# A macaron block on eight cores: layer-norm stages one round earlier, a square moved to GpSimd, attention weights staged in a buffer of their own, causal masks moved to VectorE

## The reference

```python
x = x + 0.5 * ffn(layernorm(x), W_fc, W_proj)
x = x + attn(layernorm(x), W_q, b_q, W_k, b_k, W_v, b_v, W_o, b_o)   # 16 heads of 64, causal
x = x + 0.5 * ffn(layernorm(x), W_fc, W_proj)                        # same weights

def ffn(x):
    h = square(relu(x @ W_fc.T))          # 1024 -> 4096
    y = h @ W_proj.T                      # 4096 -> 1024
    mem = 0; spikes = 0
    for _ in range(5):                    # each step needs the one before it
        reset = mem > 1
        mem = 0.9 * mem + y - reset
        spikes += mem > 1
    return spikes / 5
```

## Time and profile before

| what | value |
|---|---|
| median of 5 runs | 5807.53 us (5806.66 to 6020.43) |
| profiled execution, its own time | 5804.35 us |
| its span on the slowest core (core 6) | 5802.8 us |
| spans of the 8 cores | 5786.1 to 5802.8 us |
| busy share of PE, DVE, ACT, POOL | 66%, 32%, 37%, 5% |
| mean granted TensorE clock | 0.805 |

### The profile page before, as it was taken

One profiled execution on the slowest core, in us unless ns is written; L12 is line 12 of the kernel. 1 busy time (PEld: TensorE's weight loads), 2 busy tenths in 40 slices (PEclk: granted clock), 3 DMA queues, 4 the chain that ended last, 5 costly groups with the idle time before them and its releaser, 6 DMA issues.

```text
span 5802.8 us, 65741 instructions; the slowest of 8 cores (5786.1 to 5802.8 us)
## 1 busy us (share of the span) xinstructions
PE 3857.2 (66%) x24162; PEld 2282.6 (39%) x24194; DVE 1884.8 (32%) x2563; ACT 2150.5 (37%) x2527; POOL 262.3 (5%) x574
## 2 busy tenths in 40 slices
PE   0288888888536653666635664566663888888885
PEld 0166666666413311111113330111211666666664
DVE  0134444544421152211122115221111344445444
ACT  1134434444312213555631220446561344344443
POOL 0000000000000001111100000111110000000000
PEclk9999999999868765666767885556766999999998
DMA  4500000000030001001021001000104000000000
GB/s 173 196 15 30 15 30 30 30 27 19 22 116 15 15 1 44 29 29 29 1 88 49 16 8 44 29 10 20 29 1 152 16 30 22 24 30 30 30 15 22
DMA packets 140922, 222.38 MB, mean 38 GB/s; under 512 B 3376, under 2 KB 118064, under 8 KB 138560
## 3 DMA queue, kind: packets, MB, share of 16 engines
q1 hardware_dynamic: 116480, 117.45, 6.5%
q0 software_dynamic: 12864, 58.78, 3.0%
q10 hardware_dynamic: 11264, 41.95, 2.0%
HBM read 151.05 MB, written 67.11 MB: 38 GB/s over the span
## 4 chain that ended last, share of the span: by engine, by line
PE 41%; DVE 22%; ACT 16%; issue 10%; DMA 7%; POOL 3%; DVEq 1%; ACTq 0%; POOLq 0%; SPq 0%
PE pw L188 39%; ACT ae L989 5%; POOL ae L1014 2%; ACT f1xbf L693 2%; ACT f3xbf L693 2%; DVE f1m L689 2%; DVE f3m L689 2%; DVE f1m L684 2%; DVE f3m L684 2%; PE pw L192 2%; DVE s_cden L880 2%; DMA f1wst<-wfc 1%; ACT ae L999 1%; DVE awvu L1091 1%; ACT aq L809 1%
## 5 line engine op out<-in xcount | busy, mean ns | idle before, releaser
L188 PE MATMUL pw<-f3lnx,f3wfc 128*128 128x256 bf16 x4096 | 882.8, 285 | 122.9 <-ACT f3h L617 73.3
L188 PE MATMUL pw<-f1lnx,f1wfc 128*128 128x256 bf16 x4096 | 880.2, 284 | 123.5 <-ACT f1h L617 73.7
L188 PE MATMUL pw<-f3h,f3wpr 128*128 128x256 bf16 x4096 | 861.4, 280 | 0.4
L188 PE MATMUL pw<-f1h,f1wpr 128*128 128x256 bf16 x4096 | 859.5, 280 | 0.4
L188 PE MATMUL pw<-ae,av 128*65 128x512 bf16 (+3 forms) x1664 | 486.8, 404 | 553.7 <-POOL ae L1014 269.0
L989 ACT ACTIVATE ae<-pw,s_negc,c_f 128x1024 bf16<-128x1024 f32 x448 | 524.9, 1198 | 373.3 <-PE pw L192 301.6
L188 PEld LDWEIGHTS pw<-f3lnx,f3wfc 128*128 128x128 bf16 x4096 | 408.5, 102 | 208.5 <-issue 152.9
L188 PEld LDWEIGHTS pw<-f1lnx,f1wfc 128*128 128x128 bf16 x4096 | 407.1, 101 | 208.7 <-issue 154.0
L188 PEld LDWEIGHTS pw<-ae,av 128*65 128x65 bf16 x1664 | 164.3, 137 | 812.8 <-issue 797.2
L188 PEld LDWEIGHTS pw<-f3h,f3wpr 128*128 128x128 bf16 x4096 | 408.5, 100 | 130.1 <-issue 65.2
L188 PEld LDWEIGHTS pw<-f1h,f1wpr 128*128 128x128 bf16 x4096 | 408.2, 100 | 129.6 <-issue 64.3
(11 more groups left out here) (145 smaller groups left out, 4239.5 us busy)
## 6 DMA issues: line engine op xcount, KB each, us to landing
ax<-x1t SPq DMA_DIRECT2D x32, 1024.0 KB, 7.8
f1x<-xt SPq DMA_DIRECT2D x16, 1024.0 KB, 5.5
x1t<-f1x SPq DMA_DIRECT2D x16, 1024.0 KB, 4.6
x2t<-ax SPq DMA_DIRECT2D x16, 1024.0 KB, 6.8
f3x<-x2t SPq DMA_DIRECT2D x16, 1024.0 KB, 5.4
out<-f3x SPq DMA_DIRECT2D x16, 1024.0 KB, 4.4
f1wst<-wfc POOLq DMA_DIRECT2D x4, 2048.0 KB, 8.5
f1wst<-wfc ACTq DMA_DIRECT2D x4, 2048.0 KB, 7.9
```

What stands on the lines that cost most here:

```text
L188: sp=stop: eng.matmul(o, l, r, start=st, stop=sp))
```

## The change

There are three edits.

1. In the feed-forward stages the spike thunks are shared out over R1 to R4 (they were over R1 to R5). Stages 1 to 6 of the next tile's layer norm are emitted one round earlier, and stage 1, the square, is given to GpSimd.
2. In attention the weights pass through a new tile astg of two 1 MB halves and no longer through x_in, in the order q0, k0, q1, k1 and so on, and each cast 1 MB piece has its own dependency.
3. The two mask multiplications of each diagonal chunk go from GpSimd to VectorE.

```diff
                         if r == 1:
                             extra = stages[0]()
+                        elif r == 5:
+                            extra = stages[2]()
                         elif r == 6:
-                            extra = stages[2]()
-                        elif r == 7:
                             extra = stages[4]()
                     emit_mms(h_mms(r), y_mms(r - 1), extra,
-                             front=(r in (6, 7)))
+                             front=(r in (5, 6)))
                     relu_round(r)
-                    if pending_spike[0] and r <= 5:
-                        k_n = max(1, -(-len(pending_spike[0]) // (6 - r)))
+                    if pending_spike[0] and r <= 4:
+                        k_n = max(1, -(-len(pending_spike[0]) // (5 - r)))
...
                     if stages is not None:
-                        if r == 5:
-                            stages[1]()
+                        if r == 4:
+                            stages[1]("gpsimd")
+                        elif r == 5:
+                            stages[3]()
                         elif r == 6:
-                            stages[3]()
-                        elif r == 7:
                             stages[5]()
                             stages[6]()
```

```diff
+            astg = mksbuf(ph, "astg", [128, 2 * 2048], F32)
...
+                for idx, (nm, ddr, wt, ch) in enumerate(stjobs):
+                    pp = idx % 2
+                    sg = astg[:, pp * 2048:(pp + 1) * 2048]
+                    sgB = B(f"astg{pp}")
+                    kb.dma("gpsimd" if pp == 0 else "scalar",
...
+                    kb.op("vector", lambda e, w=wt, ch=ch, sg=sg:
+                          e.tensor_copy(
+                              w[:, ch * 2048:(ch + 1) * 2048], sg),
+                          reads=(sgB,), writes=(B(f"{nm}c{ch}"),))
...
                                 for off in (u0, 512 + u0):
-                                    kb.op("gpsimd", lambda e, off=off,
+                                    kb.op("vector", lambda e, off=off,
```

More of the change, by code:

```diff
@@ L743, in emit_attn @@
             atmp = mksbuf(ph, "atmp", [128, 2048], F32)
+            astg = mksbuf(ph, "astg", [128, 2 * 2048], F32)
+            bufs["astg0"] = Buf("astg0")
+            bufs["astg1"] = Buf("astg1")
             c_bvb = mksbuf(ph, "abvb", [1, D], BF16)
@@ L755, in emit_attn @@
                 wvb = mksbuf(qkvstack, f"awv{b}", [128, 8192], BF16)
-                for nm, ddr, wt in ((f"awq{b}", d_wq, wqb),
-                                    (f"awk{b}", d_wk, wkb),
-                                    (f"awv{b}", d_wv, wvb)):
+                for nm in (f"awq{b}", f"awk{b}", f"awv{b}"):
                     for ch in range(4):
[L760 to L771, removed]
+                        bufs[f"{nm}c{ch}"] = Buf(f"{nm}c{ch}")
@@ new lines, in emit_attn @@
+                stjobs = [(f"awq{b}", d_wq, wqb, 0), (f"awk{b}", d_wk, wkb, 0),
+                          (f"awq{b}", d_wq, wqb, 1), (f"awk{b}", d_wk, wkb, 1),
+                          (f"awq{b}", d_wq, wqb, 2), (f"awk{b}", d_wk, wkb, 2),
+                          (f"awq{b}", d_wq, wqb, 3), (f"awk{b}", d_wk, wkb, 3),
+                          (f"awv{b}", d_wv, wvb, 0), (f"awv{b}", d_wv, wvb, 1),
+                          (f"awv{b}", d_wv, wvb, 2), (f"awv{b}", d_wv, wvb, 3)]
+                for idx, (nm, ddr, wt, ch) in enumerate(stjobs):
[3 more added lines that the diff above has]
+                    kb.dma("gpsimd" if pp == 0 else "scalar",
+                           sg.rearrange("p (c n) -> p c n", c=2),
+                           ddr.ap().rearrange("(c p) n -> p c n",
+                                              p=128)[:, 2 * ch:
+                                                     2 * ch + 2, :],
+                           writes=(sgB,))
+                    kb.op("vector", lambda e, w=wt, ch=ch, sg=sg:
+                          e.tensor_copy(
+                              w[:, ch * 2048:(ch + 1) * 2048], sg),
+                          reads=(sgB,), writes=(B(f"{nm}c{ch}"),))
@@ L804, in emit_attn @@
                                           start=(dk == 0), stop=(dk == 7),
-                                          reads=(B(nm), B("alnx")))
+                                          reads=(B(f"{nm}c{dk // 2}"),
+                                                 B("alnx")))
                             for hj in range(4):
@@ L826, in emit_attn @@
                                       start=(dk == 0), stop=False,
-                                      reads=(B(f"awv{b}"), B("alnx")))
+                                      reads=(B(f"awv{b}c{dk // 2}"),
+                                             B("alnx")))
                         for hf in range(2):
@@ L930, in emit_attn @@
                     del bufs[n]
+                    for ch in range(4):
+                        del bufs[f"{n}c{ch}"]
                 corestack = ExitStack()
@@ L1206, in emit_attn @@
             for n in ("aq", "ak", "av", "ax0", "ax1", "alnx", "axbf",
-                      "axsq", "aab", "arw", "atmp", "abvb"):
+                      "axsq", "aab", "arw", "atmp", "abvb", "astg",
+                      "astg0", "astg1"):
                 del bufs[n]
```

## The result

The changed kernel has a median of 5960.37 us over 6 runs (5945.93 to 6111.47), against 5807.53 before. It is slower by a ratio of 1.0275, 95% interval 1.0213 to 1.0338. In some executions, of any kernel, the cores of a die run part of the time at a lowered clock, which lifts the medians (that of all ten executions of the kernel before to 5951.47), so single times given from here on are of executions without it: 5945.7 to 5949.3 us for this kernel, 5803 to 5807 for the one before, +140 us. The profiled execution (6016.82 us) is read on core 2 (span 5952.4 us) in f1 and attention, and on core 5 in f3, where their stores come as evenly as in the kernel before.

What follows compares the result with a forecast made beforehand. No engine is full; the spike chain's latency up to xsq's first sum sets each feed-forward tile. Feed-forward +217, masks -52, weights -15 gave +150 on 5804.35, forecast as 5956 us, range 5855 to 6050 (5905 to 6010 at 0.65).

Steps and rivals of the forecast that it cites:

- the masks' gain: Attention's diagonal chunks: masks on VectorE take 0.55 us a pair, not 1.02; -52 us in all.
- the clock given back at R0: Feed-forward, next tile's R0: without the lnx wait its matmuls no longer run at the lower clock, -2.4 us a tile.
- First sum later: Feed-forward tile: the first sum of xsq on PE starts at 1136.0, 3.7 us later than before.
- lower clock behind the long wait: Feed-forward R5: PE has stood nearly still for 14 us, so the round pays +2.4 us a tile.
- no wait for lnx: Feed-forward, next tile's R0: lnx is made during R7 and ready when wanted, -2.3 us a tile.
- The price of the square: Feed-forward square on GpSimd: 4.46 us, plus 1.1 us held by line 704 on DVE.
- dear-square rival: Feed-forward square takes 6.83 us on GpSimd and is held for all of line 704: +98 us, 6054; chance 0.12.
- Tile 0: First tile of each feed-forward stage: no Signs before it, early square, loses 7.7 us of waits and clock; twice, -15.
- 1.2 us x 48 = -58: Attention, qs = 1, 2, 3: each of 48 head pairs ends 1.2 us earlier through faster masks, -58 us.
- attention wins: Rival: PE's mask waits in attention vanish, gaining more than the feed-forward stages lose; about 5806 or 5785 us; chance 0.08.
- Head and qs = 0: Attention: masks behind W_o's casts at each core part's head cost +3, twice, +6; at qs = 0 tail_a's hold nets 0.
- Weights: Start of attention: x no longer waits for weight buffers, so statistics come 7.5 us earlier, twice, -15 us.

Runs made afterwards that it cites:

- e6: Kernel before with spike thunks shared out as 5, 4, 4, 4 and the rest over R1 to R5, one Sign per round: 5800.97 to 5806.67 us, ratio 1.0004.
- e5: Changed kernel with the square of x written to a tile of its own, xs2, instead of xsq: 5711.79 us in one execution.
- e7: Changed kernel with line 704, the store and the next load emitted behind the row statistics: 5915.13 and 5918.1 us.
- e2: Kernel before with only the mask multiplications moved from GpSimd to VectorE: 5731.16 us, ratio 0.9898.
- e3: Kernel before with only the new weight staging and its dependencies by piece: 5787.6 to 5791.6 us, ratio 0.9961.
- e9: Changed kernel with norm and spikes interleaved, square in its own tile on ScalarE, broadcasts in R4, normalising behind R4 to R7: 5252.33 and 5260.09 us.

## Why the prediction was right or wrong

The directions and the waits came as forecast. Two terms were mis-sized most, and the granted clock stands in both: the masks' gain, and the clock given back at R0. Their errors had opposite signs.

**The mechanism of edit 1 held.** The claim was that the first sum of xsq waits for the spike chain, so that a round moved from ahead of it to behind it is a round lost. The trace shows it (first sum 41.9 us behind S0, 38.2 before; line 700 34.7 us behind S0, 34.8 before), e6 shows the sum's time is not PE's to change (38.1 us with another order of waits), and e5 shows the reverse: with the square off the chain, the tile is back at 82 us.

**Term by term, a tile** (means of tiles 1 to 13 of f1, core 2). First sum later: forecast 3.7, measured 3.7. All behind it: forecast +4.6, measured 48.3 - 42.9 = +5.4. This is the mis-sized part of edit 1, +0.8 a tile, 21 us over the 26 tiles between the first and last stores:

| term behind the first sum | forecast | measured |
|---|---|---|
| one more round of 64 matmuls | +6.9 | +7.0 |
| lower clock behind the long wait | +2.4 | +2.0 (5.7 us for the 25 matmuls, 3.7 at full clock) |
| no wait for lnx | -2.3 | -2.5 |
| its lower clock gone | -2.4 | -1.1 |

The term that failed is the last, "minus 2.4 us of lower clock". It was read from one tile and taken for all. Behind the first sum the tiles before take 41.8, 43.2 or 43.3 us: three of the 13 lose nothing to the clock, six lose 1.4 us in R6, behind the 3.0 us wait that "cost no clock", and only four lose 1.5 us in R0. The price of 2.3 to 2.4 in R0 was itself too high, since it set 26 matmuls in 5.09 us against 0.107 us each, while R0's matmuls at full clock take 0.13 (39 in 5.10 us, one tile earlier).

**The price of the square was right by luck, by two errors.** Forecast 4.46 alone and 1.1 held, 5.56 us; measured 3.60 (e5, e7) and 2.11, 5.71. GpSimd is faster on one wide operation than its 128-column row and DVE's fixed part suggest, and was held for nearly all of line 704. The dear-square rival was right on the hold and wrong on the price. The Trainium skill (GPSIMD Engine Reference, Performance versus the Vector engine) gives 4497 ns for a 2048-column fp32 tensor_tensor add on GpSimd; this product of one tile with itself took 3600, and for this form the measurement decides. Its Key points say that GpSimd contends with VectorE's instructions that have two SBUF inputs; the trace agrees: 2.11 us lost beside one of 2.29.

**Tile 0** gave 4.8 us in f1 where I had 7.7. In f3 9.6 us went, but its start also holds the load of the weights, which differs by some us from core to core.

**Masks: the wrong size, and the largest miss.** Forecast -52; e2 measured -76. The step that failed is "1.2 us x 48 = -58". The 1.2 us were right as far as they went (1.28 in the pair shown). Over the 48 pairs it came to 1.8 us each in e2. What I left out is the clock: where the gap ahead of tail_pe is shorter, the broadcasts can run at 2.4 and not 1.2 GHz, 0.9 us more in the pair shown. That pair is a good one: in the mean the broadcasts won 0.3 us in e2, and the stretch ahead of them 1.5 and not 1.2. The clock of that stretch rose too, from 0.68 to 0.90, so the other 0.3 may be the clock's as well; that is argued, not isolated. I had counted the clock in the feed-forward and not here; I had it only in the rival "attention wins", which it did not bring about, as the feed-forward loss of 239 stayed more than twice attention's gain. Head and qs = 0 cost 7 us in e2 where +6 was forecast, at the places named: the first product with v came 4.0 and 4.2 us later in the two batch elements (8 cores), and at qs = 0 tail_a's wait rose by 1.0 us.

**Weights: -15 forecast**, statistics 10.2 us earlier after the barrier in the mean of the cores (7.5 forecast), -16 in e3. Of the 4 us that I took for lost to traffic, 1.2 were lost.

**The sum** missed by only 10 us by luck, because the errors had both signs: feed-forward +239 (forecast +217), attention -98.5 on core 2 (-67), -103 in the mean of the cores. My own conditions for being wrong were tiles under 83 us (they took 90.3) and core parts over 80 us shorter; per element the query blocks 1 to 3 gave 44 to 46 us.

## What to carry to other kernels

- When PE waits in several places of a loop, ask which event is set by a chain with no slack. Work moved from ahead of that event to behind it adds its full length, and a wait in front of it is worth nothing to remove (e6: 4.8 us moved, 0 won).
- A buffer that two chains share can be the tie that makes a wait. Look for it before moving work: one more tile of 4 KB per partition turned +140 us into -93 (e5), and with the norm then laid where its inputs are ready, into -552 (e9).
- Price a shorter or longer PE gap twice: once for its time, and once for the matmuls behind it at 1.2 or 2.4 GHz. Take the second price as a mean over many tiles: the same 25 matmuls behind nearly the same wait took 3.7 us in one tile and 5.15 in another.

## What the runs showed of the hardware

- A GpSimd product of two 2048-column fp32 operands (the same tile twice) into bf16 took 3.60 us alone and 5.71 beside a 2.29 us fp32 TENSOR_TENSOR on VectorE. VectorE's had started 0.04 us earlier and was not slowed. It is the other way round when GpSimd starts first: in tile 0 a VectorE operation of two fp32 rows, 0.41 us elsewhere, took 3.33 us and ended just behind the square (changed kernel, core 2; the rows stand below). In e5 the same befell line 413 of the norm (core 0: 1.97 us and not 0.43, from 411.01 to 0.28 us behind the square's end). So in these runs the later of the two waited for the earlier.
- 128-column bf16 masks took 225 ns each on VectorE (mean of 512), and two that depend on nothing but the same exp 0.55 us together; on GpSimd 427 ns mean and about 1 us for two.
- All eight cores held a granted clock of 1.00 through whole feed-forward tiles with PE busy for 99% of the time (e9, 600 to 732 us).

The square and the VectorE operation of tile 0:

```profile
246.88 3.59 POOL L359 TENSOR_TENSOR f1xsq<-f1x 128x2048 bf16<-128x2048 f32 x1 [24.41 <-PE pw L188]
247.42 3.33 DVE L376 TENSOR_TENSOR f1rw<-f1rw 1x256 f32<-1x256 f32 x1
```
